# Layer 3's output as 49 blocks, each written in two parts, the last two side by side

## The reference

```python
h = jnp.maximum(_layernorm(x, axis=-1), 0.0)
x = x + _L3_gnn_ref(h, edge_index, ...)

# _L3_gnn_ref(nodes, ...), H = 2 heads of 64
alpha = einsum('ehd,ehd->eh', q[dst], k[src]) / sqrt(64)
w     = softmax of alpha over the edges of one dst node
agg   = segment_sum(v[src] * w, dst)
x     = agg + nodes @ Wskip + bskip
gate  = sigmoid(concat([nodes, x]) @ Wgate)
fuse  = tanh(x @ Wfuse)
return gate * fuse + (1.0 - gate) * nodes
```

## Time and profile before

| | us |
|---|---|
| median of 3 runs | 5985.34 |
| lowest, highest | 5979.43, 5990.69 |
| the profiled execution's own time | 5982.85 |
| its span | 5980.8 |
| busy: PE, DVE, ACT, POOL | 4163.3, 3779.2, 1878.5, 4008.9 |

### The profile page before, as it was taken

One profiled execution on the slowest core, in us unless ns is written; L12 is line 12 of the kernel. 1 busy time (PEld: TensorE's weight loads), 2 busy tenths in 40 slices (PEclk: granted clock), 3 DMA queues, 4 the chain that ended last, 5 costly groups with the idle time before them and its releaser, 6 DMA issues. The chain is left out here.

```text
span 5980.8 us, 86128 instructions
## 1 busy us (share of the span) xinstructions
PE 4163.3 (70%) x19030; PEld 3347.1 (56%) x19030; DVE 3779.2 (63%) x11775; ACT 1878.5 (31%) x4142; POOL 4008.9 (67%) x4191
## 2 busy tenths in 40 slices
PE   4788888857676775897878887444444447777776
PEld 4677777646666664444555555333333336666665
DVE  8555555557777777646666666344444447777775
ACT  5132222233334342463333332011111124444442
POOL 2677777757777774007777777577777767777773
PEclk9987778867777776997888888555555567777776
DMA  2544444434444445165555555222222254454453
GB/s 59 135 137 119 120 118 119 117 110 141 136 139 136 137 140 128 53 288 166 155 158 158 157 159 143 60 64 68 64 68 64 68 109 144 144 150 146 144 152 64
DMA packets 426775, 738.45 MB, mean 123 GB/s; under 512 B 100522, under 2 KB 280579, under 8 KB 419700
## 3 DMA queue, kind: packets, MB, share of 16 engines
q0 software_dynamic: 173200, 436.47, 27.8%
q1 hardware_dynamic: 244484, 289.62, 14.7%
q10 hardware_dynamic: 8592, 6.82, 0.4%
HBM read 613.55 MB, written 120.20 MB: 123 GB/s over the span
## 5 line engine op out<-in xcount | busy, mean ns | idle before, releaser
L1628 POOL DMA_INDIRECT xh<-pair_d,src_i x1658 | 1582.9, 955 | 571.1 <-issue 490.4
L2659 POOL DMA_INDIRECT l2e_rows<-msg_d,msg_i x829 | 788.1, 951 | 568.2 <-POOLq L61 315.9
L854 POOL DMA_INDIRECT l2f_rows<-msg_d,msg_i x829 | 785.4, 947 | 290.1 <-issue 239.2
L999 POOL DMA_INDIRECT l0e_rows<-node_d,src_i x829 | 789.8, 953 | 260.3 <-issue 222.9
L1156 PE MATMUL l0e_ps<-l0e_rows,l0e_sel 128*128 128x256 f32 x1664 | 712.0, 520 | 193.8 <-DVE early_acc L1223 76.4
L888 PE MATMUL l2f_ps<-l2f_rows,l2f_sel 128*128 128x128 f32 x1664 | 427.3, 423 | 579.6 <-DVE l2f_sel L907 359.9
L888 PEld LDWEIGHTS l2f_ps<-l2f_rows,l2f_sel 128*128 128x128 f32 x1664 | 372.5, 315 | 661.9 <-DVE l2f_sel L907 399.5
L2793 PE MATMUL l2e_ps<-l2e_rows,l2e_sel 128*128 128x256 f32 x1664 | 550.6, 461 | 80.6 <-DVE l2e_sel L2885 38.2
L1223 DVE TENSOR_TENSOR early_acc<-early_acc,l0e_ps 128x264 f32 x832 | 356.3, 428 | 335.8 <-PE l0e_ps L1157 262.1
L919 DVE TENSOR_TENSOR xh<-xh,l2f_ps 128x128 f32 x832 | 238.8, 287 | 519.3 <-PE l2f_ps L888 413.1
L2850 DVE TENSOR_TENSOR l_acc<-l_acc,l2e_ps 128x256 f32 x832 | 349.1, 420 | 325.5 <-PE l2e_ps L2793 321.8
(11 more groups left out here) (463 smaller groups left out, 8336.5 us busy)
## 6 DMA issues: line engine op xcount, KB each, us to landing
l0e_rows<-in_edge_attr_dram SPq DMA_DIRECT2D x832, 64.0 KB
msg_d<-l1t_queries SPq DMA_DIRECT2D x50, 1024.0 KB, 3.9
l1te_local<-local_d SPq DMA_DIRECT2D x52, 512.0 KB
l2e_local<-local_d SPq DMA_DIRECT2D x52, 512.0 KB
l3te_local<-local_d SPq DMA_DIRECT2D x52, 512.0 KB
xh<-pair_d,src_i POOLq DMA_INDIRECT x1658, 2.8
msg_d<-l2e_msg SPq DMA_DIRECT2D x50, 512.0 KB
l0e_rows<-node_d,src_i POOLq DMA_INDIRECT x829
```

The lines of the kernel that those rows point to most:

```text
L854: pool.indirect_dma_start(rows[:, t % R, :], None, table, bass.IndirectOffsetOnAxis(index[:, t:t + 1], 0)) \
L999: pool.indirect_dma_start(rows[:, t % R, 0:D], None, table, bass.IndirectOffsetOnAxis(g.src_i[:, t:t + 1], 0)).then_inc(gathered[t % R], 16)
L1628: pool.indirect_dma_start(rows[:, t % R, :], None, g.pair_d, bass.IndirectOffsetOnAxis(g.src_i[:, t:t + 1], 0)).then_inc(gathered[n % RG], 16)
L2659: pool.indirect_dma_start(rows[:, t % R, :], None, table, bass.IndirectOffsetOnAxis(index[:, t:t + 1], 0)).then_inc(gathered[t % R], 16)
```

## The change

- `survey` breaks ties between windows of as many tiles the other way round (the window's number is subtracted instead of added). Window 49 keeps rank 0 and the last one rank 49.
- The empty window gets no block. EACH = 49; block k is the window of rank k + 1.
- Every block is written in two parts. Its last TAIL = 22 rows go out first, to the row number clamped to N - 128, plus 106; SP waits until that has landed (`ended`); then its first HEAD = 106 rows go to the window's own place. For the last window the first part falls on rows that its own head (and nothing later) covers. The two repeated blocks are gone, and with them the wait for all earlier stores.
- SP loads two table entries for each store instead of one.
- LAG = 8: blocks 0 to 46 lie in the steps. Blocks 47 and 48 are interleaved behind the steps, 47 with a second set of buffers (in `wide`, which is free by then) and a second PSUM bank; both tails are sent first, then one wait, then both heads.
- `fetch` loads three blocks at a time throughout (the last load one block).

```diff
@@ survey
-    size = size * P + g.iota
+    size = size * P - g.iota          # scalar_tensor_tensor, ALU.add -> ALU.subtract
@@ class Outputs
-    EACH = NW + 2
+    EACH = NW - 1
-    LOADS = -(-NW // FEW) + 1
+    LOADS = -(-EACH // FEW)
+    SIDE = EACH - 2
+    HEAD, TAIL = REST, P - REST
+    TOP = N - P
...
+    def aside(self, k):
+        return 1 if k == self.SIDE else 0
+
+    def back(self, k):
+        return 0 if k == self.SIDE else k - 1 if k == self.SIDE + 1 else k
...
     def store(self, sp, k):
         if k == 0:
-            sp.wait_ge(self.clamped, 1)
-        if k < NW:
-            v = windows_of(self.nc, self.g, mybir.EngineType.SP, k + P // 2, count=1, at=2 * TA, top=LASTW - 1)[0]
-            sp.wait_ge(self.done, k + 1)
-            sp.dma_start(self.out[bass.ds(v * P, P), :], self.res[:, k % 2, :]).then_inc(self.sent[k % 2], 16)
-            return
-        if k == NW:
-            for one in self.sent:
-                sp.wait_ge(one, 16 * (NW // 2))
-        v = LASTW - 1 + k - NW
-        rows = min(P, N - v * P)
+            sp.wait_ge(self.placed, 1)
+        v = self.window(mybir.EngineType.SP, k)
+        row = windows_of(self.nc, self.g, mybir.EngineType.SP, k + 1 + P // 2, count=1, at=2 * TA, top=self.TOP)[0]
         sp.wait_ge(self.done, k + 1)
-        sp.dma_start(self.out[v * P:v * P + rows, :], self.res[0:rows, k % 2, :]).then_inc(self.sent[k % 2], 16)
+        sp.dma_start(self.out[self.HEAD:N, :][bass.ds(row, self.TAIL), :],
+                     self.res[self.HEAD:P, k % 2, :]).then_inc(self.ended, 16)
+        sp.wait_ge(self.ended, 16 * (k + 1))
+        sp.dma_start(self.out[bass.ds(v * P, self.HEAD), :], self.res[0:self.HEAD, k % 2, :]).then_inc(self.sent[k % 2], 16)
+
+    def store_pair(self, sp, k):
+        two = (k, k + 1)
+        vs = [self.window(mybir.EngineType.SP, i) for i in two]
+        rows = [windows_of(...)[0] for i in two]
+        for i, row in zip(two, rows):
+            sp.wait_ge(self.done, i + 1)
+            sp.dma_start(self.out[self.HEAD:N, :][bass.ds(row, self.TAIL), :],
+                         self.res[self.HEAD:P, i % 2, :]).then_inc(self.ended, 16)
+        sp.wait_ge(self.ended, 16 * (k + 2))
+        for i, v in zip(two, vs):
+            sp.dma_start(self.out[bass.ds(v * P, self.HEAD), :], self.res[0:self.HEAD, i % 2, :]).then_inc(self.sent[i % 2], 16)
...
@@ attention_edges
-    LAG = 7
+    LAG = 8
...
 # SP, behind the steps
-                    for k in range(NS - LAG - 2, o.EACH):
+                    for k in range(NS - LAG - 2, o.EACH - 2):
                         o.store(sp, k)
                         o.fetch_after(sp, k)
+                    o.store_pair(sp, o.EACH - 2)
                     o.land(sp)
...
 # PE, behind the steps
-                    for k in range(NS + 3 - LAG, o.EACH):
+                    pe.wait_ge(used, NS * GS)
+                    for k in (o.SIDE, o.SIDE + 1):
                         o.turn(pe, k)
+                    for k in (o.SIDE, o.SIDE + 1):
                         o.mix(pe, k)
+                    for k in (o.SIDE, o.SIDE + 1):
                         o.gate(pe, k)
...
 # ACT, behind the steps
-                    o.squash(act, NS + 2 - LAG)
-                    for k in range(NS + 3 - LAG, o.EACH):
+                    o.squash(act, o.SIDE - 1)
+                    act.wait_ge(looked, NS * GS)
+                    for k in (o.SIDE, o.SIDE + 1):
                         o.share(act, k)
                         o.move(act, k)
+                    for k in (o.SIDE, o.SIDE + 1):
                         o.shift(act, k)
+                    for k in (o.SIDE, o.SIDE + 1):
                         o.squash(act, k)
...
 # DVE, behind the steps
                     dve.wait_ge(added, T)
-                    for k in range(NS + 2 - LAG, o.EACH):
-                        if k >= NS + 3 - LAG:
-                            o.cap(dve, k)
-                            o.invert(dve, k)
+                    for k in (o.SIDE, o.SIDE + 1):
+                        o.cap(dve, k)
+                    for k in (o.SIDE, o.SIDE + 1):
+                        o.invert(dve, k)
+                    for k in range(o.SIDE - 1, o.EACH):
                         o.take_apart(dve, k)
                         o.weigh(dve, k)
                         o.finish(dve, k)
```

More of the change, by code:

```diff
@@ L1388, in __init__ @@
+        self.gates, self.diff = [st.sb("o_gates", [P, 2, D])], [st.sb("o_diff", [P, 2, D])]
         self.res = st.sb("o_res", [P, 2, D])
[L1389 to L1393, removed]
+        self.po = [st.ps("o_po")]
@@ L1395, in __init__, with beside @@
         self.sent = [sem(f"l3o_sent{b}") for b in range(2)]
-    def window(self, engine, k):
-        return window_of(self.nc, self.g, engine, k) if k < NW else LASTW - 1 + k - NW
+    def beside(self, room, bank):
+        self.z.append(room[:, 0, :])
+        self.ht.append(room[:, 1, :])
+        self.xt.append(room[:, 2, :])
+        self.gates.append(room[:, 3:5, :])
+        self.diff.append(room[:, 5:7, :])
+        self.po.append(bank)
+    def window(self, engine, k):
+        return windows_of(self.nc, self.g, engine, k + 1, count=1, at=2 * TA, top=LASTW)[0]
@@ L1425, in fetch @@
             sp.wait_ge(self.done, self.FEW * (j - 1))
[L1426 to L1429, removed]
-            return
[L1431 to L1437, removed]
+        first, n = j * self.FEW, min(self.FEW, self.EACH - j * self.FEW)
+        sp.dma_start(self.pairs[j % 2][:, 0:n, :, :].rearrange("p w k f -> p (w k f)"),
+                     self.g.late_d[:, (first + 1) * 2 * D:(first + 1 + n) * 2 * D]).then_inc(self.landed[j % 2], 16)
     def fetch_after(self, sp, k):
@@ new lines, in store @@
+        sp.wait_ge(self.ended, 16 * (k + 1))
[3 more added lines that the diff above has]
+        vs = [self.window(mybir.EngineType.SP, i) for i in two]
+        rows = [windows_of(self.nc, self.g, mybir.EngineType.SP, i + 1 + P // 2, count=1, at=2 * TA, top=self.TOP)[0]
+                for i in two]
+        for i, row in zip(two, rows):
[5 more added lines that the diff above has]
+            sp.dma_start(self.out[bass.ds(v * P, self.HEAD), :], self.res[0:self.HEAD, i % 2, :]).then_inc(self.sent[i % 2], 16)
@@ L1459, in land @@
     def land(self, sp):
-        for one in self.sent:
-            sp.wait_ge(one, 16 * (self.EACH // 2))
+        for b in range(2):
+            sp.wait_ge(self.sent[b], 16 * len(range(b, self.EACH, 2)))
     def share(self, act, k):
-        nc = self.nc
+        nc, b = self.nc, self.aside(k)
         v = self.window(mybir.EngineType.Activation, k)
         act.wait_ge(self.shared, k + 1)
-        if k >= 1:
-            act.wait_ge(self.mixed, k)
+        if self.back(k) >= 1:
+            act.wait_ge(self.mixed, self.back(k))
@@ L1471, in share @@
             act.nop(nofuse=True)
-            ins = nc.scalar.activation(self.z[:, at:at + D // self.H], self.acc[:, self.part(v, at, D // self.H)],
-                                       ACT.Copy, scale=self.den[:, h:h + 1])
+            ins = nc.scalar.activation(self.z[b][:, at:at + D // self.H], self.acc[:, self.part(v, at, D // self.H)],
+                                       ACT.Copy, scale=self.den2[:, b, h:h + 1])
         ins.then_inc(self.evened, 1)
     def part(self, v, at, n):
-        return bass.ds(v * self.AW + at, n) if not isinstance(v, int) else slice(v * self.AW + at, v * self.AW + at + n)
+        return bass.ds(v * self.AW + at, n)
@@ L1489, in squash @@
     def squash(self, act, k):
         act.wait_ge(self.gated, k + 1)
[L1491 to L1494, removed]
+        if self.back(k) >= 1:
+            act.wait_ge(self.weighed, self.back(k))
+        self.nc.scalar.activation(self.gates[self.aside(k)][:, :, :].rearrange("p k f -> p (k f)"),
+                                  self.po[self.aside(k)][:, 0:2 * D], ACT.Tanh).then_inc(self.acted, 1)
@@ L1604, in attention_edges @@
         pw = [st.ps(f"pw{b}") for b in range(2)]
+        if late:
+            o.beside(wide[:, 0, :, :], pq[0])
         px = [pw[b][:, 0:2 * P].rearrange("p (k s h) -> p k s h", k=2, h=HS) for b in range(2)]
```

75 lines of the change are left out of this document (40 added, 35 removed).

## The result

| | before | after |
|---|---|---|
| median of 13 runs each, us | 5992.21 | 6002.84 |
| lowest, highest | 5979.43, 5996.87 | 5990.93, 6009.90 |
| span of the profiled execution | 5980.8 | 5999.8 |
| layer 3's edges, first gather to last addition | 1104.1 | 1131.5 |
| from the last addition to the end of the span | 29.8 | 14.2 |

A forecast was written before the change was run, and what follows sets the result against it. GpSimd's gathers set the pace at 20.0 us a step, with 1.2 us of cushion for late indices. 5982.85 + 90 (steps) - 14 (end) = 6059, so 6061 at the median of runs; range 5990 to 6115.

The forecast's parts named there:

- the end: Behind layer 3's last steps: the interleaved pair gives its result 17.2 us earlier, the last store costs more; -14 us.
- the loop's term: Layer 3's steps: indices issued 3.4 us later, less 1.2 us of slack, 2.2 us in 41 steps; +90 us.
- the cushion: Delay a step can take before GpSimd's gathers lose the pace; 1.2 us, from DVE's waits for gathers.
- the ring: One turn a step: SP issues indices, then ACT, PE's sums, DVE's `fell`, and SP's next indices; 20.9 us.
- load, wait and resumption: SP's queue between `fell` and indices: second register load 0.5 us, landing of 22 rows 2.2, resumption and address 0.1.
- narrow head in place of the store: The 106-row write uses two DMA engines and holds the indices' packets queued behind it; 0.6 us a step.
- Rival C: The 106-row write on two engines is the main cost, 4.2 us a step, +172 - 14, 6143 us; 15%.
- What was said to show it: Signs: ACT waits 5 to 7 us for indices, SP about 2, GpSimd 2 a step; DVE's near zero; steps 22 us.
- Ties, one block fewer, LAG: Window order in all layers: zero, give or take 3 us; 47 blocks in the steps for 48: nothing.
- A: Rival: GpSimd's gathers keep the pace, steps stay at 20.0 us, only the end counts; 5971 us, 12%.
- B: Rival: the cushion is 3 us or so, 16 us lost in the steps and 14 gained; 5987 us, 8%.
- D: Rival: the pair at the end is no faster, waiting for the result buffer; gains 5, not 14; 6070 us, 5%.

The follow-up runs named there:

- e9: The kernel before with a 22-row write to an unused buffer, waited for, ahead of the store in 42 steps: 5997.30 us, ratio 1.0027.
- e3: The kernel before with only the ties of the window ranking reversed: 5983.16 us against 5984.05, ratio 1.0.
- e2: The changed kernel with whole 128-row stores, a last block of 106 rows and no wait for tails: 5962.86 us, ratio 0.9971 to before.
- e7: The changed kernel with wait and head of each store moved behind the issue of the next step's indices: 5966.43 us, ratio 0.9972 to before.
- e1: The changed kernel with both parts of each store in the steps sent without the wait between them: 5964.13 us, ratio 0.9968 to before.
- e5: The kernel before with one 22-row write to an unused buffer, waited for, behind each store in the steps: 5988.83 us, ratio 1.0011.
- e6: The kernel before with two 22-row writes to an unused buffer, each waited for, behind each store in the steps: 6068.53 us, ratio 1.014.

## Why the prediction was right and wrong

The direction, the mechanism and the end were right, the size was not. **The step that failed is the loop's term: "Sum 0.5 + 2.2 + 0.1 + 0.6 = 3.4 us later in every step", less "the cushion of 1.2 us", 2.2 us a step times 41, +90 us.** The mechanism is as forecast; this term was put too large in its push and too small in its cushion. It measured 0.68 us a step and +27.4 us. The account by its own parts, from the table of the ring:

| us a step | forecast | measured |
|---|---|---|
| load, wait and resumption | 2.8 | 2.12 (4.22 - 2.10) |
| narrow head in place of the store | 0.6 | 0.11 (5.18 - 5.07) |
| first sum to `fell` | 0 | 0.10 |
| slack used up | 1.2 | 1.59 (1.73 - 0.14) |
| step | +2.2 | +0.7 |

- *The wait.* The head goes out 1.98 us after the tail in the mean of the 41 steps (1.46 to 4.36), where wait and resumption were put at 2.3. That is nearer to the lower of its two bounds, 1.5 us for idle engines, than to the upper, 2.8: the loaded landing of a gather was a poor model for 22 rows on SP. One such write is 33 packets, 22 rows and 11 completions (5986 to 5987.65), the 11 engines of the prediction.
- *The load.* From `fell` to the store's issue it is 1.82 us for 1.51, +0.30 us for a load put at 0.5; the other 1.82 of the 2.12 are the 1.98 less the shorter way from the head's issue to the indices (0.43 us for 0.58 from the store's). The 0.49 us of the earlier trace rows is what a load takes that stands alone. In the kernel after they stand in pairs, and of 41 pairs (5000 to 5900) the first takes 0.53 us and the second 0.27.
- *The narrow head.* 0.6 was twice what it costs beyond a store of 128 rows just ahead (0.3 by e9), and in the kernel before that store already stood there. Rival C fell with it.
- *The cushion.* Its floor was read from one row of two steps, 0.5 us; where the ring binds it is 0.12 to 0.15 in six kernels. And DVE's waits for gathers, taken as the generous value, were the smaller one: 1.2 against 1.59. A difference of nearly equal sums carries the whole error of each of its terms: three were off by 0.4 to 0.7 us, all to the same side, and with the 0.1 against them they took 1.5 of 2.2.
- *What was said to show it.* ACT's wait of 5 to 7 us a step came (5.3), SP's wait came (1.5 for about 2), DVE's wait for gathers went to near zero (6.1 us in all). GpSimd's wait of 2 us a step did not (28.9 us in 42 steps, 0.7), nor the step of 22 us (21.03). That ACT's wait grew by 2.0 us a step and the step by 0.7 is no contradiction: the rest of the lateness was taken from the slack.
- *The end.* Forecast -14, measured -15.6. The 1.6 us lie in the pair: from the gates of the block ahead of it to the last result 8.2 us were forecast, and it is 6.7 (5986.82 to 5993.55). PE's part of that, from block 48's mix to its last gate, is 3.45 us for 4.6. From the result to the end 6.1 was forecast, measured 6.25. Behind the last addition 14.2 us are left where some 16 were said. The rate of the two heads is that of one, as forecast.
- *Ties, one block fewer, LAG.* Nothing, as forecast (e3, e2).
- *The rivals.* A, that GpSimd keeps the pace, fell: the ring binds. B, a larger cushion with 16 us lost in the loop and 14 gained, 5987, is nearest to what happened, but partly by luck: its cushion of 3 us was too large and its push of 3.4 too, 1.59 and 2.3 in their place. D fell: the end gained 15.6 us and not 5.
- *The rule that was weighed.* 2.0 us for the fixed cost of a DMA, which the Trainium skill gives in "DMA: Bandwidth & Descriptors", "Anatomy of one DMA — SWDGE (gpsimd) path", is close to the 1.98 us between tail and head in the steps here, though the queue is SP's. With few other transfers it is 1.43 us here, so it is not constant. In the forecast it would have been a little nearer than my 2.2.

## What to carry to other kernels

A wait in a queue that issues DMAs costs what stands behind it: before adding one, put the load that the next step needs ahead of it, as e7 does by order alone. And where two paces are nearly equal, measure the slack directly, as the gap between the last input that is ready and the instruction that uses it, in many steps: below the slack a delay costs nothing (e1: 0.75 us later, steps 20.34 for 20.35; e7), above it all of it (e5 to e6, 1.83 us of step for 1.85 of delay), so a doubt of half a microsecond is a doubt of 20 us in 41 steps.

## What had not been expected of the hardware

- 22 rows written by SP and waited for take 1.43 us from issue to the next issue with few other transfers (5986.27 to 5987.70 in the drain after the last gathers) and 1.98 us in the mean in the loaded stage: half a microsecond more, though the DMA engines are busy for 0.47 of the time there (4900 to 5900).
- With a narrow write of 1.4 us of traffic just ahead of it, the wide load of the indices reached ACT only 0.3 us later than behind a 128-row store (5.18 against 4.88, between kernels that differ in more than this).
- A table load on SP takes 0.49 us alone and 0.27 us as the second of two; the pair added 0.30 us to the queue.
